# Taking the softmax remainder two pairs at a time, with the weighing four pairs behind the scores

## The chip, the cores and the metric

One core of one Trainium2 chip runs the whole program. The metric is device microseconds (us) of one execution. TensorE is called PE here, VectorE DVE, ScalarE ACT, GpSimd POOL, and SyncE, which issues most of the DMAs, SP.

## The reference

Two graph layers over 4096 rows of 128 features, each with a residual and a layernorm:

```
norm2 = ||x|| by row                              # (4096, 1)
cos   = beta * (x @ x.T) / (norm2 @ norm2.T + 1e-7)
P     = softmax(cos + (1 - adj) * -1e9, axis=1)   # adj: 4096 x 4096 of 0 and 1, with its diagonal
x     = layernorm(x + P @ x)
x     = layernorm(x + adj @ (x @ weight))
```

## The kernel before

The first layer works in 8 blocks of 512 output rows (`b`), and in each block over the 4096 columns of the graph in 16 **pairs** of 128-column tiles (`m`); `n = 16 b + m` counts the 128 pairs. Everything is held transposed: one pair is a tile of 128 partitions by 2 x 512 columns. Sums run in float16 with a high part and a remainder ("lo"), so that they keep the precision of float32. For one pair:

1. `scores(b, m)` on PE: six matmuls of 512 columns (L854 to L856) into one of two PSUM buffers `S`. It waits until the exponential of pair n-2 has been taken.
2. `exp_pair` on ACT (L424): `E[slot] = exp(scale * S)`, float32, 1024 columns. `E`, `eh` and `el` are rings of RING = 4 slots, one for each pair. It waits for the remainder of pair n-4 (`lo_done`), which still reads the slot of `E`.
3. `mask_pair` on DVE (L639): E times a power of two, minimum with the bytes of the transposed adjacency (`adjT`), in place.
4. `split_hi` on ACT (L433): `eh[slot]` = E in float16. It waits for the weighing of pair n-4 (`pv_done`).
5. `split_lo` on DVE (L647): `el[slot]` = E minus `eh`, in float16: the **remainder**.
6. `weigh` on PE (L877, L881): sixteen matmuls, eight of 257 columns with `eh` and eight of 129 with `el`, add the pair into the four PSUM banks `O`. It waits for `lo_done` of the pair.

Each engine runs its own program in the order in which it is written, and waits on semaphores between. In one step `m` PE does `scores(b, m)` and then `weigh` of the pair LAG = 3 behind; ACT does `exp_pair(b, m)` and then `split_hi(b, m-1)`; DVE does `mask_pair(b, m)` and then `split_lo(b, m-1)`.

The end of block b-1 is worked in among the steps of block b. At step LAG, ACT copies a part of `O` out (`read_out`, L449) and DVE adds the rest (L685, `o_read`); PE weighs nothing at that step's turn and, one step later, weighs pair 0 (which waits for `o_read`) and pair 1. DVE then spreads small instructions over the steps: `scale_den` at step 3, `residual` (L698) at 4 and 5, `row_moments` (L652) at 6 and 7, `norm_stats` (L659 to L677) at 8. POOL takes a power (`power`, L376) of what `norm_stats` leaves, and DVE's `row_shift` (L709) at step 10 waits for it. ACT's `normalise` (L460), one tile at each of the steps 11 to 14, waits for `row_shift` before its first tile, and `split_x1_hi` (L469) at step 15 lets POOL subtract the high part of the result (`x1p`, L388).

POOL also starts the DMAs that turn the float32 adjacency into bytes in DRAM (`cast`, L353), and its queue is served in order, so a `power` stands behind the casts in front of it. SP transposes the bytes into `adjT` (L258, L264). Each of the two waits for the other's last pieces.

The second layer starts when the last pair is weighed: `aggregate` (L935) on PE, 64 fp8/float16 matmuls of 512 columns for each block, and `weights` (L945). At the end of the first layer PE weighs the last LAG pairs one after the other and goes straight to `aggregate`.

Of the kernel before, what the change touches and what calls it, by code (L numbers as in the profile page):

```python
# [11 lines left out]
ALU = mybir.AluOpType  # L12
# [9 lines left out]
def resnorm_graph_kernel(nc, x, adj, beta, weight, x1_dram, x1p_dram, q_dram, adj8_dram, out):  # L22
# [10 lines left out]
    NT = N // P  # L33
    NP = NT // 2
    NPAIR = NB * NP
    LAG = 3
    RING = 4
    XC = 2 * D + 1
    HB = BI // 2
# [11 lines left out]
    with ExitStack() as ctx:  # L51
# [3 lines left out]
        def sem(name):  # L55
            return ctx.enter_context(nc.semaphore(name))
# [101 lines left out]
        lo_done = sem("lo_done")  # L158
# [238 lines left out]
        def _(act):  # L397
# [43 lines left out]
            def read_out(b):  # L441
                if later(b):
                    act.wait_ge(o_read, 2 * b)
                for half in range(2):
                    if half == 0:
                        act.wait_ge(half_weighed, b + 1)
                    else:
                        act.wait_ge(pv_done, (b + 1) * NP)
                    nc.scalar.activation(o_lo[:, half * HT:(half + 1) * HT, :],  # L449
                                         psum[:, 4 + half * HT:4 + (half + 1) * HT, D:XC],  # L450
                                         ACT.Copy).then_inc(o_lo_read, 1)
# [28 lines left out]
            for b in range(1, NB):  # L480
                for m in range(NP):
                    if m == LAG:
                        read_out(b - 1)
# [25 lines left out]
        def _(dve):  # L509
# [24 lines left out]
            def uT_lo_part(g):  # L534
                dve.wait_ge(uT_hi, g + 1)
                nc.vector.tensor_tensor(uT_out(1, g), uT_in(g), uT_out(0, g), ALU.subtract).then_inc(uT_lo, 1)
# [61 lines left out]
            def add_small_term(b, m):  # L598

                n = b * NP + m  # L600
                dve.wait_ge(s_filled, n + 1)
                dve.wait_ge(q_row_in, 16 * (b + 1))
                if later(b) or m >= RING:
                    dve.wait_ge(lo_done, n - RING + 1)
                for a in range(2):
                    num, den = E[:, m % RING, a, 0:HB], E[:, m % RING, a, HB:BI]
                    for half in range(2):
                        base = 16 * n + 8 * a + 4 * half
                        part = slice(half * HB, (half + 1) * HB)
                        rows = q_row[:, part].rearrange("q (r p) -> q p r", r=2)  # L610
                        nc.vector.tensor_scalar_mul(num.rearrange("q (p r) -> q p r", r=2), rows,
                                                    q[:, 2 * m + a:2 * m + a + 1]).then_inc(fix, 1)
                        dve.wait_ge(fix, base + 1)
                        nc.vector.tensor_scalar_add(den, num, EPS_COS).then_inc(fix, 1)
                        dve.wait_ge(fix, base + 2)
                        nc.vector.reciprocal(den, den).then_inc(fix, 1)
                        dve.wait_ge(fix, base + 3)
                        nc.vector.tensor_tensor(num, num, den, ALU.mult).then_inc(fix, 1)
                        dve.wait_ge(fix, base + 4)
                        s = S[m % 2][:, a, part]  # L620
                        done = nc.vector.tensor_tensor(s, s, num, ALU.mult)
                        if half == 0:
                            done.then_inc(half_scaled, 1)
                            dve.wait_ge(half_scaled, 2 * n + a + 1)
                        elif a == 1:
                            done.then_inc(scaled, 1)

            def mask_pair(b, m):

                n = b * NP + m  # L630
                dve.wait_ge(e_done, n + 1)
                if not later(b) and m < 3:
                    dve.wait_ge(first_in[m], 16)
                elif m == 0:
                    dve.wait_ge(piece_in[0], 16 * b)
                elif m % (NP // MP) == 0:
                    dve.wait_ge(piece_in[m // (NP // MP)], 16 * (b + 1))
                e = E[:, m % RING, :, :]
                nc.vector.scalar_tensor_tensor(out=e, in0=e, scalar=EPRE, in1=mask_bytes(b, m), op0=ALU.mult,  # L639
                                               op1=ALU.min).then_inc(masked, 1)  # L640

            def split_lo(b, m):

                n = b * NP + m
                dve.wait_ge(hi_done, n + 1)
                s = m % RING
                nc.vector.scalar_tensor_tensor(out=el[:, s, :, :], in0=E[:, s, :, :], scalar=ECAST, in1=eh[:, s, :, :],  # L647
                                               op0=ALU.mult, op1=ALU.subtract).then_inc(lo_done, 1)

            def moments(src, o, ts, base):  # L650
                for t in ts:
                    last = nc.vector.bn_stats(stats[:, o + t, :], src(t))  # L652
                if IT - 1 in ts:
                    last.then_inc(chain, 1)
# [38 lines left out]
            def residual(b, ts):  # L693
                dve.wait_ge(o_read, 2 * (b + 1))
                dve.wait_ge(chain, 6 * b + 2)
                dve.wait_ge(xres_in, 16 * (b + 1))
                for t in ts:
                    last = nc.vector.scalar_tensor_tensor(out=h[:, t, :], in0=h[:, t, :], scalar=rden[:, t:t + 1],  # L698
                                                          in1=xres[:, t, :], op0=ALU.mult, op1=ALU.add)
                if IT - 1 in ts:  # L700
                    last.then_inc(chain, 1)

            def row_moments(b, ts):
                dve.wait_ge(chain, 6 * b + 3)
                moments(lambda t: h[:, t, :], 0, ts, 6 * b + 3)
# [11 lines left out]
            def xaug_lo(c):  # L717
                dve.wait_ge(x_hi, c + 1)
                nc.vector.scalar_tensor_tensor(out=xaug[:, chunk(c), D + 1:XC], in0=xfull[:, chunk(c), :],
                                               scalar=col(C_XS), in1=xaug[:, chunk(c), 0:D], op0=ALU.mult,  # L720
                                               op1=ALU.subtract).then_inc(x_lo, 1)

            def layer(tiny):
                for m in range(NP):
                    if tiny:
                        add_small_term(0, m)
                    mask_pair(0, m)
                    if m % 2 == 0 and m < 2 * NC:
                        xaug_lo(m // 2)
                    if m in (1, 2):  # L730
                        uT_lo_part(UG // 2 + 2 * m - 2)
                        uT_lo_part(UG // 2 + 2 * m - 1)
                    if m > 0:
                        split_lo(0, m - 1)
                def block_of_rows(b):
                    for m in range(NP):
                        if m == LAG:
                            read_out(b - 1)
                        if tiny:
                            add_small_term(b, m)  # L740
                        mask_pair(b, m)
                        split_lo(b, m - 1)
                        if m == 3:
                            scale_den(b - 1)
                        if m in (4, 5):
                            residual(b - 1, range(2 * m - 8, 2 * m - 6))
                        if m in (6, 7):
                            row_moments(b - 1, range(2 * m - 12, 2 * m - 10))
                        if m == 8:
                            norm_stats(b - 1)  # L750
                        if m == 10:
                            row_shift(b - 1)

                if tiny:
                    with dve.Fori(1, NB) as b:
                        block_of_rows(b)
                else:
                    for b in range(1, NB):
                        block_of_rows(b)
                split_lo(NB, -1)  # L760

            with dve.If(small < 1):
                layer(False)
# [3 lines left out]
            b = NB - 1  # L767
# [56 lines left out]
        def _(pe):  # L824
# [69 lines left out]
            def weigh_lagged(b, m):  # L894
                weigh(b * NP + m - LAG, (m - LAG) % NP)

            for m in range(NP):
# [11 lines left out]
                if m == 0:  # L909
                    pe.wait_ge(norms, 1)  # L910
                    pe.wait_ge(uT_lo, 4)
                    nc.tensor.transpose(q_turned, q[:, :], ident[:, :]).then_inc(q_filled, 1)
                if m == LAG:

                    pe.wait_ge(uT_lo, UG)
                if m >= LAG:
                    if (m - LAG) % (CT // 2) == 0:
                        pe.wait_ge(x_lo, (m - LAG) // (CT // 2) + 1)
# [74 lines left out]
```

## Time and profile before

| | |
|---|---|
| time, median of 3 runs | 515.58 us (515.1 to 516.22) |
| the profiled execution's own time | 515.68 us |
| its span in the profile | 513.8 us |
| busy: PE, DVE, ACT, POOL | 469.7, 380.6, 314.2, 64.8 us |
| first layer's pairs | to about 389 us |
| second layer | from about 389 us |

The profiled execution lies 0.1 us from the median, so its trace can stand for the runs. Busy times are over the whole span; DVE and ACT have little to do in the second layer, where PE works alone. In the rows further down a start is in us from the span's start, and the idle time in brackets is that of the row's own engine before the instruction, with what ended it.

### The profile page before, as it was taken

The numbers are of one execution on the slowest core, as the hardware profiler recorded it, in microseconds if no ns is written. First come the engines' busy times: TensorE is split into PE (matmuls) and PEld (weight loads), VectorE is DVE, ScalarE is ACT, GpSimd is POOL, SyncE is SP. The second block draws the span as 40 slices with busy tenths as digits, with TensorE's granted clock in tenths as the row PEclk, the third lists the DMA queues.
The fourth block names the chain that finished last, engine by engine and source line by source line (L and its number), as shares of the span: only waits on it lengthen the run. The fifth ranks groups of instructions, "written<-read, shape, count | busy, mean of one in ns | idle before, by whom it ended". The sixth has DMA issues, their size and how long they took to land.

```text
span 513.8 us, 8872 instructions
## 1 busy us (share of the span) xinstructions
PE 469.7 (91%) x3491; PEld 305.1 (59%) x3491; DVE 380.6 (74%) x630; ACT 314.2 (61%) x358; POOL 64.8 (13%) x71
## 2 busy tenths in 40 slices
PE   0866999957999999999999999999999999999995
PEld 0533676635676666766666767666665455544584
DVE  4976989928999999999999999999994022212253
ACT  3665888828879978988988997898891000000000
POOL 3500000010101201201120210110101000000011
PEclk9988999997999999999999999999999999999998
DMA  5899899999999999999989979520024101111111
GB/s 189 62 101 127 86 122 115 137 127 115 172 127 135 131 136 118 131 169 115 112 171 114 105 152 104 93 74 7 1 51 156 63 5 37 41 43 41 42 37 46
DMA packets 101690, 50.20 MB, mean 98 GB/s; under 512 B 69376, under 2 KB 98208, under 8 KB 101664
## 3 DMA queue, kind: packets, MB, share of 16 engines
q0 software_dynamic: 17952, 16.78, 39.5%
q1 hardware_dynamic: 83424, 33.05, 30.2%
q8 instruction: 11, 0.18, 0.1%
q14 instruction: 15, 0.12, 0.1%
q10 hardware_dynamic: 288, 0.07, 0.1%
HBM read 77.40 MB, written 22.82 MB: 195 GB/s over the span
## 4 chain that ended last, share of the span: by engine, by line
PE 66%; DMA 20%; DVE 4%; issue 4%; ACT 3%; POOL 1%; POOLq 0%; ACTq 0%; DVEq 0%
PE psum L935 21%; PE psum L877 16%; DMA adj_bytes<-in_adj 12%; PE psum L881 8%; DMA adjT<-adj_bytes 7%; PE psum L854 7%; PE psum L856 7%; PE psum L855 7%; DVE E L639 2%; ACT E L424 1%; PE psum L945 1%; DMA adjT<-in_x 1%; ACT eh L433 1%; DVE el L647 1%; POOL rn L360 1%
## 5 line engine op out<-in xcount | busy, mean ns | idle before, releaser
L877 PE MATMUL psum<-xaug,eh 128*128 128x257 f16 x1024 | 187.9, 277 | 22.5 <-DVE el L647 15.4
L424 ACT ACTIVATE E<-psum,sc 128x1024 f32<-128x1024 f32 x128 | 154.1, 1204 | 54.8 <-PE psum L856 50.6
L881 PE MATMUL psum<-xaug,el 128*128 128x129 f16 x1024 | 178.7, 223 | 0.0
L639 DVE SCALAR_TENSOR_TENSOR E<-E,adjT 128x1024 f32<-128x1024 f32 x128 | 160.0, 1250 | 21.1 <-ACT E L424 13.0
L647 DVE SCALAR_TENSOR_TENSOR el<-E,eh 128x1024 f16<-128x1024 f32 x128 | 156.5, 1223 | 0.1
L433 ACT ACTIVATE eh<-E 128x1024 f16<-128x1024 f32 x128 | 134.0, 1047 | 3.8 <-DVE E L639 3.8
L877 PEld LDWEIGHTS psum<-xaug,eh 128*128 128x128 f16 x1024 | 100.3, 99 | 52.3 <-DVE el L647 16.9
L935 PE MATMUL psum<-adjT,uT 128*128 128x512 fp8e4 (+1 forms) x576 | 112.1, 355 | 0.0
L881 PEld LDWEIGHTS psum<-xaug,el 128*128 128x128 f16 x1024 | 101.4, 99 | 13.4
L854 PE MATMUL psum<-uT 128*128 (+1 forms) x256 | 98.4, 384 | 0.0
L855 PE MATMUL psum<-uT 128*128 (+1 forms) x256 | 97.8, 382 | 0.0
L856 PE MATMUL psum<-uT 128*128 (+1 forms) x256 | 97.5, 381 | 0.0
L935 PEld LDWEIGHTS psum<-adjT,uT 128*128 128x128 f16 x576 | 56.4, 98 | 53.0
L501 ACT ACTIVATE E<-psum 128x512 f32<-128x512 f32 x7 | 4.2, 597 | 88.0 <-PE psum L935 88.0
L792 DVE TENSOR_TENSOR E<-psum,E 128x512 f32<-128x512 f32 x7 | 4.8, 690 | 68.1 <-PE psum L945 68.1
L376 POOL TENSOR_TENSOR rstd<-rstd,half_pow 128x4 f32<-128x4 f32 (+1 forms) x17 | 22.2, 1304 | 186.1 <-DVE rstd L677 186.1
L353 POOL DMA_DIRECT2D adj_bytes<-in_adj x31 | 19.6, 631 | 192.1 <-DMA adjT<-adj_bytes 192.1
L856 PEld LDWEIGHTS psum<-uT 128*128 128x128 f16 x256 | 25.3, 99 | 31.0 <-issue 1.4
L854 PEld LDWEIGHTS psum<-uT 128*128 128x128 f16 x256 | 25.4, 99 | 17.9 <-issue 0.7
L855 PEld LDWEIGHTS psum<-uT 128*128 128x128 f16 x256 | 25.3, 99 | 16.4 <-issue 0.5
L460 ACT ACTIVATE x<-h,shift,rstd 128x128 f32<-128x128 f32 x32 | 15.2, 482 | 16.6 <-DVE shift L709 16.6
L388 POOL TENSOR_TENSOR x1p<-x,x1p 128x512 f16<-128x512 f32 x7 | 12.4, 1764 | 58.6 <-ACT x1p L469 58.6
(71 smaller groups left out, 159.9 us busy)
## 6 DMA issues: line engine op xcount, KB each, us to landing
adj_bytes<-in_adj POOLq DMA_DIRECT2D x31, 512.0 KB, 11.1
adjT<-in_x SPq DMA_DIRECT2D x4, 512.0 KB, 8.6
xres<-in_x SPq DMA_DIRECT2D x8, 256.0 KB, 5.3
q_row<-norms SPq DMA_DIRECT2D x8, 256.0 KB, 4.9
x_rows<-x SPq DMA_DIRECT2D x8, 256.0 KB, 3.6
E<-x_rows SPq DMA_DIRECT2D x8, 256.0 KB, 3.0
out<-E SPq DMA_DIRECT2D x16, 128.0 KB, 2.2
x_parts<-x1p SPq DMA_DIRECT2D x7, 256.0 KB, 5.5
```

The lines of the kernel that those rows point to most:

```text
L353: pool.dma_start(piece(adj8_v, b, c), piece(adj_v, b, c)).then_inc(piece_cast[c], 16)
L376: nc.gpsimd.tensor_tensor(rstd[:, o:o + n], rstd[:, o:o + n], half_pow[:, 0:n], ALU.pow).then_inc(rstd_done, 1)
L424: nc.scalar.activation(E[:, m % RING, :, :], S[m % 2], ACT.Exp, bias=col(C_BB), scale=col(C_BS)).then_inc(e_done, 1)
L433: nc.scalar.activation(eh[:, m % RING, :, :], E[:, m % RING, :, :], ACT.Copy, scale=ECAST).then_inc(hi_done, 1)
L639: nc.vector.scalar_tensor_tensor(out=e, in0=e, scalar=EPRE, in1=mask_bytes(b, m), op0=ALU.mult, op1=ALU.min).then_inc(masked, 1)
L647: nc.vector.scalar_tensor_tensor(out=el[:, s, :, :], in0=E[:, s, :, :], scalar=ECAST, in1=eh[:, s, :, :], op0=ALU.mult, op1=ALU.subtract). ...
L854: nc.tensor.matmul(o, hj, hi, start=True, stop=False)
L855: nc.tensor.matmul(o, hj, li, start=False, stop=False)
L856: last = nc.tensor.matmul(o, lj, hi, start=False, stop=True)
L877: return nc.tensor.matmul(O[t][:, 0:XC], eh[:, s, a, cols], xaug[:, j, :], start=start, stop=stop)
L881: return nc.tensor.matmul(O[t][:, 0:D + 1], el[:, s, a, cols], xaug[:, j, 0:D + 1], start=False, stop=False)
L935: last = nc.tensor.matmul(out, x1p_all[:, j, part * D:(part + 1) * D], adj_cols(r, j, cols), start=j == 0 and part == 0, stop=j == NT - 1 ...
```

## The change

`LAG` goes from 3 to 4, while the rings keep 4 slots. `split_lo` now takes the remainder of two pairs in one instruction of 2048 columns, at even steps only: at step m (even) it covers pairs m-2 and m-1, and raises `lo_done` by 2. The small instructions of the row end are set to other steps: `scale_den` 4, `residual` 5 and 7, `row_moments` 8 and 9, `norm_stats` 9, `row_shift` 11. `read_out` moves with LAG, from step 3 to 4, on ACT and on DVE, and so do PE's empty turn (4) and double turn (5). ACT's `normalise` stays at steps 11 to 14.

```
-    LAG = 3
+    LAG = 4
     RING = 4
...
                 dve.wait_ge(hi_done, n + 1)
-                s = m % RING
+                s = slice((m - 1) % RING, (m - 1) % RING + 2)
                 nc.vector.scalar_tensor_tensor(out=el[:, s, :, :], in0=E[:, s, :, :], scalar=ECAST, in1=eh[:, s, :, :],
-                                               op0=ALU.mult, op1=ALU.subtract).then_inc(lo_done, 1)
+                                               op0=ALU.mult, op1=ALU.subtract).then_inc(lo_done, 2)
...
-                    if m > 0:
+                    if m > 0 and m % 2 == 0:
                         split_lo(0, m - 1)
...
                         mask_pair(b, m)
-                        split_lo(b, m - 1)
-                        if m == 3:
+                        if m % 2 == 0:
+                            split_lo(b, m - 1)
+                        if m == 4:
                             scale_den(b - 1)
-                        if m in (4, 5):
-                            residual(b - 1, range(2 * m - 8, 2 * m - 6))
-                        if m in (6, 7):
-                            row_moments(b - 1, range(2 * m - 12, 2 * m - 10))
-                        if m == 8:
+                        if m in (5, 7):
+                            residual(b - 1, range(m - 5, m - 3))
+                        if m in (8, 9):
+                            row_moments(b - 1, range(2 * m - 16, 2 * m - 14))
+                        if m == 9:
                             norm_stats(b - 1)
-                        if m == 10:
+                        if m == 11:
                             row_shift(b - 1)
```

## Rows read from the trace of the kernel before

**Rows 1.** The page's groups: busy us, mean ns, then idle before and its releaser.

```profile
L639 DVE SCALAR_TENSOR_TENSOR E<-E,adjT 128x1024 f32<-128x1024 f32 x128 | 160.0, 1250 | 21.1 <-ACT E L424 13.0
L647 DVE SCALAR_TENSOR_TENSOR el<-E,eh 128x1024 f16<-128x1024 f32 x128 | 156.5, 1223 | 0.1
...
L698 DVE SCALAR_TENSOR_TENSOR h<-h,rden,xres 128x128 f32<-128x128 f32 x32 | 9.6, 345 | 0.1
...
L685 DVE TENSOR_TENSOR h<-psum,o_lo 128x256 f32<-128x256 f32 x16 | 6.0, 416 | 3.6 <-issue 3.6
```

**Rows 2.** Who waited for whom: us in total, times, longest us.

```profile
PE psum L877 <- DVE el L647: 15.4, 4, 8.9
...
PE psum L877 <- DVE h L685: 2.3, 7, 0.9
```

**Rows 3.** The chain that ended last, in pieces: start us, us, what.

```profile
118.44 0.40 PE psum L877
...
304.03 0.23 PE psum L856
...
346.60 0.23 PE psum L856
...
385.30 2.06 DVE el L647
...
388.92 27.69 PE psum L935 x128
```

**Rows 4.** Timeline of PE: a weighing after a wait, and one followed by scores.

```profile
46.92 0.39 PE L877 MATMUL psum<-xaug,eh 128*128 128x257 f16 x1 [4.86 <-DVE el L647]
...
290.90 0.27 PE L877 MATMUL psum<-xaug,eh 128*128 128x257 f16 x1
...
292.24 0.38 PE L854 MATMUL psum<-uT 128*128 x1
```

**Rows 5.** Timeline of ACT: the exponential and the first normalised tile.

```profile
116.14 0.49 ACT L460 ACTIVATE x<-h,shift,rstd 128x128 f32<-128x128 f32 x1 [9.51 <-DVE shift L709]
116.54 1.19 ACT L424 ACTIVATE E<-psum,sc 128x1024 f32<-128x1024 f32 x1
...
291.24 1.20 ACT L424 ACTIVATE E<-psum,sc 128x1024 f32<-128x1024 f32 x1
...
299.15 1.21 ACT L424 ACTIVATE E<-psum,sc 128x1024 f32<-128x1024 f32 x1
...
381.65 1.21 ACT L424 ACTIVATE E<-psum,sc 128x1024 f32<-128x1024 f32 x1
```

**Rows 6.** Timeline of DVE: masks, remainders and the row end.

```profile
43.31 1.23 DVE L639 SCALAR_TENSOR_TENSOR E<-E,adjT 128x1024 f32<-128x1024 f32 x1 [7.67 <-DMA adjT<-adj_bytes]
...
115.95 0.16 DVE L709 SCALAR_TENSOR_TENSOR shift<-mean,rstd 128x4 f32<-128x4 f32 x1 [10.27 <-POOL rstd L376]
...
117.16 1.22 DVE L647 SCALAR_TENSOR_TENSOR el<-E,eh 128x1024 f16<-128x1024 f32 x1
118.30 1.22 DVE L639 SCALAR_TENSOR_TENSOR E<-E,adjT 128x1024 f32<-128x1024 f32 x1
...
279.13 0.48 DVE L652 BATCH_NORM_STATS2 stats<-h 128x6 f32<-128x128 f32 x2
...
281.79 0.15 DVE L659 TENSOR_TENSOR tmp<-stats 128x4 f32<-128x4 f32 x1
...
282.56 1.22 DVE L639 SCALAR_TENSOR_TENSOR E<-E,adjT 128x1024 f32<-128x1024 f32 x1
...
300.38 1.83 DVE L639 SCALAR_TENSOR_TENSOR E<-E,adjT 128x1024 f32<-128x1024 f32 x1 [0.27 <-ACT E L424]
```

**Rows 7.** Timeline of POOL: a power, and the remainder of the result.

```profile
114.87 1.04 POOL L376 TENSOR_TENSOR rstd<-rstd,half_pow 128x4 f32<-128x4 f32 x1
...
299.27 1.86 POOL L388 TENSOR_TENSOR x1p<-x,x1p 128x512 f16<-128x512 f32 x1 [12.16 <-ACT x1p L469]
```

**Rows 8.** Windows of 1 us, one of them: busy by engine, granted clock (PEclk), DMA.

```profile
47.00:48.00 1.00, 1.00 (x7) 0.81 (x8) 1.00 (x2) 0.76 (x1) 0.00 (x0) 0.50 1.06 93
```

## The prediction, on record before the changed kernel ran

> **What bounds the kernel now.** I read the page first, then the waits, the chain, the windows, and last the timelines of each engine around a block's end. The page shows DVE busy at every pair, yet with idle time in front of the masks that ACT's exponential ended 13.0 us of [rows 1]: DVE is not the bound of the steady part. The pace is PE's. Exponentials run three pairs apart at 291.24 and 299.15, 2.637 us a pair [rows 5]; a weighing takes 292.24 - 290.90 = 1.34 [rows 4], which leaves 1.30 for the scores, and PE is at work all that time. From block to block the chain repeats every 346.60 - 304.03 = 42.57 us [rows 3], that is 16 x 2.637 = 42.19 and 0.38 in which PE waits for DVE's read-out (seven such waits, 2.3 us, the longest 0.9 [rows 2]). Time not spent at this pace lies at the start, where casts and transposes come late: a mask waits 7.67 us for its DMA at 43.31, and at 115.95 `row_shift` has waited 10.27 us for POOL's power [rows 6], which started at 114.87 [rows 7], right behind a cast that a DMA held. PE starts again at 118.44 [rows 3]. So three things can matter: what DVE's new order makes PE wait for, the read-out, and the end of the layer.
>
> **The merged instruction, by itself.** Two remainders that follow without a wait start 1.14 apart (117.16 to 118.30 is one remainder and the next mask) [rows 6]. From 128 to 1024 columns such an instruction grows by 1223 - 345 = 878 ns over 896 columns [rows 1], or 1.00 us for 1024 more: 2.14 us from start to next start. With no saving at all it would be 2.28. I take 2.20, the middle. At best this frees 64 x 0.14 = 9 us of DVE, at worst none, and none of it lies on the path: while PE sets the pace it is worth 0. If DVE were the bound, that would be the gain. Here a rule speaks against the change: the Trainium skill, "Perfetto Trace Analysis", section "Optimizing Scalar/DVE Operations", says that grouping helps a saturated engine, with about 60 ns of access overhead for each DVE operation, and that breaking instructions up may finish work sooner where the engine isn't saturated but holds another up. By its 60 ns the merge would give 64 x 0.06 = 3.8 us if DVE were saturated and nothing as it is; the trace agrees that DVE is not.
>
> **The steady pace.** Call X(n) the start of exp n. The mask follows after 1.23 (299.15 to 300.38), the double remainder 1.14 later, and PE can weigh 1.28 + 1.06 = 2.34 after its start (117.16 to 118.44 was 1.28 [rows 3, 6]). The first of the two pairs is ready at X(n) + 4.71. PE wants it at X(n+2) less 0.34 (290.90 against 291.24 [rows 4, 5]) = 4.93. It holds, by 0.22 us. That is all the slack there is: DVE late by more than this at an even step stalls PE.
>
> **Blocks 2 to 7, steps 8 to 14: the loss.** The row end now falls so that a chain passes through DVE, ACT and DVE again. From X(8): mask 8 at 1.23, remainder (6, 7) at 2.37, over at 4.57; `row_moments` 0.48 [rows 6], 5.05; mask 9, 6.19; `row_moments` 0.48 and `norm_stats` 0.77 (281.79 to 282.56), 7.44; this is 0.94 late for mask 10, whose exp is ready at 5.27 + 1.23 = 6.50. Mask 10, 8.58; remainder (8, 9), 10.78; mask 11, 11.92; only now `row_shift`. ACT has exp 12 behind `normalise`, which waits for that: 0.19 to the tile, 0.40 to exp 12 (115.95, 116.14, 116.54 [rows 5, 6]), 12.51. DVE has nothing between, since step 11 is odd. Mask 12 at 13.74, remainder (10, 11) at 14.88, PE can weigh pair 10 at 17.22. PE wants it at 6 x 2.637 - 0.34 = 15.48. The stall is 1.74 us (0.6 of it already before pair 8). With 2.14 and 2.28 for the three double remainders it is 1.56 and 1.98. After it there is slack again: exp 14 to 16 and normalise fit in PE's pace. Before the change `row_shift` stood one step earlier, with a remainder behind it, and cost nothing. Six blocks: **+10.4** (9.4 to 11.9). POOL's power starts one step later, still some 3 us ahead of `row_shift`; the casts behind it move by as much, and after block 2 no mask waits for them. SP's queue waits for masks and for x1, not for remainders.
>
> **Block ends.** While POOL subtracts x1p (299.27, 1.86 us [rows 7]) the mask at 300.38 takes 1.83 instead of 1.22 [rows 6]. That was hidden. Now it is mask 16, an even one, so pairs 14 and 15 are ready at 1.23 + 1.75 + 2.34 = 5.32, against 4.93: 0.39 us, in five blocks **+2.0**. Bounds: 0, if POOL's instruction falls elsewhere, and 3, if it lies over more.
>
> **The read-out** moves a step later, and PE gets the scores of one more pair in front of the weighing that waits. From X(2): remainder (0, 1) over at 4.57, mask 3 at 5.71, read-out 0.42 [rows 1], 6.13; PE wants it at 5.27 - 0.34 + 1.30 = 6.23. No wait: five blocks give back 0.38, block 2 its 0.9: **-2.8** (at least -2.3).
>
> **The start.** In block 0 the mask at 43.31 now has two remainders behind it, one of which (pair 2) had been taken earlier. PE resumes 1.06 later and with a weighing of 1.34 undone: 2.4 us late. But block 1 ends at POOL's power, at 115.95, which hangs on DMAs, and PE was idle for 8.9 us there [rows 2]. The delay goes into that idle time. From there: exp 12 at 116.54 as before, scores 14 at once at half clock (as behind the idle time at 46.92: clock 0.50 [rows 4, 8]), mask 12, the remainder of 10 and 11, PE's weighing of 10 at about 121.3, done 122.6. Before, both were done at 122.6 too. **0** (to +1, if the clock comes back later).
>
> **The end of the layer.** Before, from the last exp at 381.65 to the first `aggregate` at 388.92 it took 7.27 [rows 3, 5]. Now, from X(127): the remainder (124, 125) is over at 4.57 - 2.64 = 1.93, the mask runs from there, and the last remainder starts 2.41 after the mask's start (before: 382.88 to 385.30) or when POOL's x1p is over: the row at 385.30 took 2.06, 0.84 too long, which puts that at 4.49. PE weighs pair 126 at 6.83, then 1.34 and 1.51 for the last: 9.68, less 1.34 because one weighing more lies behind the last scores. **+1.1** (0.8 to 1.4). PE idles about 3.1 us there; 4.9 us idle brought half the clock [rows 4, 8]. If 3.1 do so too, 1.5 more.
>
> **Sum:** 10.4 + 2.0 - 2.8 + 0 + 1.1 = +10.7 on the profiled execution's 515.68: **526.4 us**. Median and profiled execution differ by 0.1.
>
> **Rivals.** (a) *Faster.* PE feels nothing of the chain through `row_shift`, and what shows is the read-out: 515.7 - 2.8 + 1.1 = 514.0. It decides if the 17.22 fall below 15.48. Every link has a duration in the trace and the order of both engines forbids going round it. 4 in 100. (b) *A smaller loss.* Mask 10 isn't late, since DVE's small instructions close up, and x1p misses mask 16: the stall is 1.74 - 0.94 = 0.80, six times 4.8, in all 515.7 + 4.8 - 2.8 + 1.1 = 518.8. Against it stands that `row_moments` and `norm_stats` have those times in the rows. 11 in 100, of which 3 for no measurable change. (c) *A larger loss.* The sync at 115.95 does not absorb the 2.4 us of the start, because DMAs wait for compute after all, and the clock falls at the layer's end: 526.4 + 2.4 + 1.5 = 530.3, more if x1p takes 3. For it: nothing in SP's or POOL's queue before 115 that I find. 10 in 100. (d) *The merge doesn't shorten DVE's work*: in the range (1.98 a block). The forecast itself has 75.
>
> **Range.** The bounds of the terms give 9.4 + 0 - 2.8 + 0 + 0.8 = +7.4 and 11.9 + 3 - 2.3 + 1 + 1.4 = +15.0. I widen the low end toward (b): 520.5 to 531. A measurement can tell about 0.2%, 1 us. Slower 93 in 100, same 3, faster 4.
>
> **What would show it.** Block period in the chain about 44.3 us instead of 42.57. PE waits for L647 rise by six stalls of 0.6 and of 1.1 us and five of 0.4. Exp 12 waits for `shift` L709 in blocks 2 to 7, and mask 12 for exp 12, about 1.8 us each. PE's waits for L685 go to about nothing after block 1. The power at about 115 keeps its time. L647: 64 instructions of about 2.3 us. Wrong would be: no wait at exp 12, a steady part that is no longer at 2.637 a pair, or a first resumption of PE after 119.

## The result, and the profile after

The changed kernel takes 524.38 us (median of 4 runs, 523.47 to 526.12) against 515.34 us for the kernel before: ratio 1.0183, 95% interval 1.0146 to 1.022. It is slower by 9.0 us, where 10.7 was forecast. The profiled execution took 523.47, with a span of 521.7.

The page's groups for the changed kernel. PE's lines have moved by one (L877 is L878 now):

```profile
L878 PE MATMUL psum<-xaug,eh 128*128 128x257 f16 x1024 | 187.0, 276 | 23.2 <-DVE el L647 21.9
L639 DVE SCALAR_TENSOR_TENSOR E<-E,adjT 128x1024 f32<-128x1024 f32 x128 | 157.7, 1232 | 39.3 <-ACT E L424 31.8
...
L647 DVE SCALAR_TENSOR_TENSOR el<-E,eh 128x2048 f16<-128x2048 f32 x64 | 146.2, 2285 | 1.2 <-ACT eh L433 1.2
```

The 64 double remainders save 10.3 us of DVE's busy time against [rows 1], and DVE waits 18.8 us longer for exponentials. Who waited for whom (us, times, longest):

```profile
DVE E L639 <- ACT E L424: 31.8, 43, 1.7
ACT x L460 <- DVE shift L709: 26.2, 8, 8.4
...
PE psum L878 <- DVE el L647: 21.9, 18, 5.7
```

PE waited for remainders 4 times before [rows 2], 18 times now. The chain, in pieces (start us, us, what), gives the block's period and the start of `aggregate`:

```profile
279.24 0.23 PE psum L857
...
323.10 0.23 PE psum L857
...
396.85 27.63 PE psum L936 x128
```

A block takes 43.86 us, 1.67 over PE's 42.19, against 42.57 before [rows 3]; `aggregate` starts 7.93 later. Timeline of DVE at steps 8 to 12 of one block, and around mask 16:

```profile
284.21 0.48 DVE L652 BATCH_NORM_STATS2 stats<-h 128x6 f32<-128x128 f32 x2
284.61 1.21 DVE L639 SCALAR_TENSOR_TENSOR E<-E,adjT 128x1024 f32<-128x1024 f32 x1
285.73 0.48 DVE L652 BATCH_NORM_STATS2 stats<-h 128x6 f32<-128x128 f32 x2
...
287.02 1.22 DVE L639 SCALAR_TENSOR_TENSOR E<-E,adjT 128x1024 f32<-128x1024 f32 x1
288.16 2.29 DVE L647 SCALAR_TENSOR_TENSOR el<-E,eh 128x2048 f16<-128x2048 f32 x1
290.36 1.22 DVE L639 SCALAR_TENSOR_TENSOR E<-E,adjT 128x1024 f32<-128x1024 f32 x1
291.50 0.15 DVE L709 SCALAR_TENSOR_TENSOR shift<-mean,rstd 128x4 f32<-128x4 f32 x1
293.31 1.23 DVE L639 SCALAR_TENSOR_TENSOR E<-E,adjT 128x1024 f32<-128x1024 f32 x1 [1.66 <-ACT E L424]
294.45 2.29 DVE L647 SCALAR_TENSOR_TENSOR el<-E,eh 128x2048 f16<-128x2048 f32 x1
...
301.50 1.22 DVE L639 SCALAR_TENSOR_TENSOR E<-E,adjT 128x1024 f32<-128x1024 f32 x1
303.65 1.23 DVE L639 SCALAR_TENSOR_TENSOR E<-E,adjT 128x1024 f32<-128x1024 f32 x1 [0.93 <-ACT E L424]
```

ACT in the same block, and the last exponential of the layer:

```profile
291.69 0.49 ACT L460 ACTIVATE x<-h,shift,rstd 128x128 f32<-128x128 f32 x1 [2.00 <-DVE shift L709]
292.09 1.19 ACT L424 ACTIVATE E<-psum,sc 128x1024 f32<-128x1024 f32 x1
...
387.51 1.21 ACT L424 ACTIVATE E<-psum,sc 128x1024 f32<-128x1024 f32 x1 [0.32 <-PE psum L857]
```

And PE: the two restarts that belong to those steps (pairs 8 and 10), with the read-out wait of block 2 in front.

```profile
138.45 0.28 PE L878 MATMUL psum<-xaug,eh 128*128 128x257 f16 x1 [1.24 <-DVE h L685]
...
290.50 0.29 PE L878 MATMUL psum<-xaug,eh 128*128 128x257 f16 x1 [0.51 <-DVE el L647]
...
296.79 0.29 PE L878 MATMUL psum<-xaug,eh 128*128 128x257 f16 x1 [0.85 <-DVE el L647]
```

In the kernel before, the same links stood like this (DVE, then ACT): the mask follows `row_shift` at once, and the tile at 288.02 comes 0.9 us after it and has not waited.

```profile
287.10 0.15 DVE L709 SCALAR_TENSOR_TENSOR shift<-mean,rstd 128x4 f32<-128x4 f32 x1
287.21 1.23 DVE L639 SCALAR_TENSOR_TENSOR E<-E,adjT 128x1024 f32<-128x1024 f32 x1
...
288.02 0.48 ACT L460 ACTIVATE x<-h,shift,rstd 128x128 f32<-128x128 f32 x1
```

In the changed kernel this is the chain to read in order: mask 11 at 290.36, `row_shift` at 291.50, the normalised tile at 291.69, exp 12 at 292.09, mask 12 at 293.31, double remainder at 294.45, PE at 296.79. DVE stands idle for 1.66 us in the middle of it. The same two waits, 0.51 and 0.84 or 0.85 us, stand in each of blocks 2 to 7; each restart loses a little more than the idle time shown, 1.67 in all by the period.

### The profile page after: what moved, and what is told of

It is laid out like the page before. It is cut to its first block, busy times and chain, and to the rows that moved or that the text cites. A ratio compares the mean times of both kernels' runs of the same rounds, so it can differ in the third digit from the quotient of the medians.

```text
span 521.7 us, 8878 instructions
## 1 busy us (share of the span) xinstructions
PE 474.0 (91%) x3491; PEld 304.8 (58%) x3491; DVE 373.2 (72%) x566; ACT 313.3 (60%) x358; POOL 60.9 (12%) x71
## 4 chain that ended last, share of the span: by engine, by line
PE 54%; DMA 20%; DVE 16%; ACT 4%; issue 4%; POOL 1%; POOLq 0%; ACTq 0%; DVEq 0%
PE psum L936 21%; PE psum L878 12%; DMA adj_bytes<-in_adj 11%; DVE el L647 9%; DMA adjT<-adj_bytes 8%; PE psum L882 6%; PE psum L857 5%; PE psum L855 5%; PE psum L856 5%; DVE E L639 4%; ACT E L424 4%; PE psum L946 1%; DMA adjT<-in_x 1%; DVE stats L652 1%; POOL rn L360 1%
## 5 line engine op out<-in xcount | busy, mean ns | idle before, releaser
L878 PE MATMUL psum<-xaug,eh 128*128 128x257 f16 x1024 | 187.0, 276 | 23.2 <-DVE el L647 21.9
L639 DVE SCALAR_TENSOR_TENSOR E<-E,adjT 128x1024 f32<-128x1024 f32 x128 | 157.7, 1232 | 39.3 <-ACT E L424 31.8
L647 DVE SCALAR_TENSOR_TENSOR el<-E,eh 128x2048 f16<-128x2048 f32 x64 | 146.2, 2285 | 1.2 <-ACT eh L433 1.2
L878 PEld LDWEIGHTS psum<-xaug,eh 128*128 128x128 f16 x1024 | 100.0, 99 | 56.6 <-DVE el L647 25.7
L855 PE MATMUL psum<-uT 128*128 (+1 forms) x256 | 99.4, 388 | 5.1 <-ACT E L424 5.1
L856 PE MATMUL psum<-uT 128*128 (+1 forms) x256 | 99.2, 388 | 0.0
L857 PE MATMUL psum<-uT 128*128 (+1 forms) x256 | 99.0, 387 | 0.0
L833 PE MATMUL psum<-ident,adjT 128*128 128x128 f32 x32 | 6.6, 367 | 12.1 <-DVE adjT L530 12.1
```

The source lines that it names most:

```text
L855: nc.tensor.matmul(o, hj, hi, start=True, stop=False)
L856: nc.tensor.matmul(o, hj, li, start=False, stop=False)
L857: last = nc.tensor.matmul(o, lj, hi, start=False, stop=True)
L878: return nc.tensor.matmul(O[t][:, 0:XC], eh[:, s, a, cols], xaug[:, j, :], start=start, stop=stop)
```

## The experiments

Each was run beside the kernel before; ratios are to its runs on the same chip: 515.81 us in the median for the first four experiments, 514.65 for the last four. So times of the two groups are compared by their ratios. "A block" is one of blocks 2 to 7, by its period less 42.19 (the kernel before: 0.38).

**`row_shift` back at step 10.** One step of the changed kernel is edited.

```
-                        if m == 11:
+                        if m == 10:
                             row_shift(b - 1)
```

> The changed kernel with row_shift back at step 10, behind the double remainder (8, 9); nothing else moves. Theory A (the chain that holds exp 12 behind row_shift behind mask 11 makes most of the loss, on top of mask 10 being late): exp 12 starts about 0.9 us late instead of 1.8, the stall in front of pair 10 goes, that in front of pair 8 (0.5 to 0.7) stays; each of blocks 2 to 7 loses 0.7 instead of 1.67, so 524.4 - 5.8 = about 518.6 us. Rival B (the double remainder by itself makes PE wait, wherever the row end stands): 524, as the changed kernel. Rival C (only the late mask 10 costs, exp 12 is hidden): 524, as the changed kernel.

518.82 us, ratio 1.0052 (1.0021 to 1.0084). PE's timeline, two blocks in a row:

```profile
288.34 0.28 PE L878 MATMUL psum<-xaug,eh 128*128 128x257 f16 x1 [0.51 <-DVE el L647]
...
331.18 0.28 PE L878 MATMUL psum<-xaug,eh 128*128 128x257 f16 x1 [0.50 <-DVE el L647]
```

Only the wait before pair 8 is left, at a period of 42.84: 0.65 a block, 1.02 less than in the changed kernel. B and C fall for the wait before pair 10; whether the double remainder by itself causes the wait before pair 8 is left to the fourth experiment. More than half of the loss was `row_shift` standing one step too late.

**`normalise` one step later.** The same link, cut on ACT; DVE's order is the changed kernel's.

```
-                    if m in (11, 12, 13, 14):
-                        normalise(b - 1, [m - 11])
+                    if m in (12, 13, 14, 15):
+                        normalise(b - 1, [m - 12])
```

> The changed kernel with ACT's normalise at steps 12 to 15 instead of 11 to 14; DVE's order stays. Theory A: exp 12 no longer stands behind row_shift, so the stall in front of pair 10 goes, that in front of pair 8 stays (0.5 to 0.7), and ACT is up to 0.4 late at exp 16 (0.15 us of PE): about 0.85 a block instead of 1.67, so 519.5 us. The same link as in the run with row_shift at step 10, cut on the other engine. Rivals B and C: 524.

518.63 us, ratio 1.0058 (1.0034 to 1.0083). DVE's timeline shows the gap behind `row_shift` closed:

```profile
288.64 0.15 DVE L709 SCALAR_TENSOR_TENSOR shift<-mean,rstd 128x4 f32<-128x4 f32 x1
288.91 1.23 DVE L639 SCALAR_TENSOR_TENSOR E<-E,adjT 128x1024 f32<-128x1024 f32 x1
```

and PE's the wait before pair 8, 43.10 apart, 0.91 a block where 0.85 was expected:

```profile
287.64 0.28 PE L878 MATMUL psum<-xaug,eh 128*128 128x257 f16 x1 [0.51 <-DVE el L647]
...
330.74 0.28 PE L878 MATMUL psum<-xaug,eh 128*128 128x257 f16 x1 [0.51 <-DVE el L647]
```

What exceeds the 0.65 of the run above comes before pair 14: exp 16 starts 3.11 after exp 15 (295.89 to 299.00), and the double remainder behind it is late.

**The merge alone undone.** LAG 4 and the new steps stay.

```
-                s = slice((m - 1) % RING, (m - 1) % RING + 2)
+                s = m % RING
...
-                                               op0=ALU.mult, op1=ALU.subtract).then_inc(lo_done, 2)
+                                               op0=ALU.mult, op1=ALU.subtract).then_inc(lo_done, 1)
...
-                    if m > 0 and m % 2 == 0:
+                    if m > 0:
...
-                        if m % 2 == 0:
-                            split_lo(b, m - 1)
+                        split_lo(b, m - 1)
```

> The changed kernel with the merge alone undone: one remainder of 1024 columns at each step, LAG 4 and every small instruction where the changed kernel has it. Theory A: a single remainder is ready 3.9 us before PE wants it, so a late exp 12 and a late mask 10 cost nothing, and the read-out's wait stays away; against the kernel before: -1.9 (blocks 3 to 7), -0.9 (block 2), -1.3 (a weighing more lies behind the last scores), -0.6 (scores 14 start on exp 12 at the sync): about 511 us. Rival D (the new places of the row end cost by themselves, on ACT, merged or not): 520 or more.

521.44 us, ratio 1.0115 (1.0089 to 1.0142): a miss by 10 us, and rival D holds. PE waits for no remainder in blocks 2 to 7, as theory A had it, but its wait for the read-out has grown from 0.24 to 1.32. DVE's timeline:

```profile
249.55 0.15 DVE L709 SCALAR_TENSOR_TENSOR shift<-mean,rstd 128x4 f32<-128x4 f32 x1
251.35 1.23 DVE L639 SCALAR_TENSOR_TENSOR E<-E,adjT 128x1024 f32<-128x1024 f32 x1 [1.65 <-ACT E L424]
...
261.19 1.91 DVE L639 SCALAR_TENSOR_TENSOR E<-E,adjT 128x1024 f32<-128x1024 f32 x1 [0.20 <-ACT E L424]
263.02 1.21 DVE L647 SCALAR_TENSOR_TENSOR el<-E,eh 128x1024 f16<-128x1024 f32 x1
...
270.97 0.74 DVE L685 TENSOR_TENSOR h<-psum,o_lo 128x256 f32<-128x256 f32 x2
```

and PE's: the weighing that waits for it:

```profile
271.44 0.28 PE L877 MATMUL psum<-xaug,eh 128*128 128x257 f16 x1 [1.32 <-DVE h L685]
```

The 1.65 us behind `row_shift` are the same. The remainders then have slack, but the read-out of the next block, eight instructions of DVE after mask 16, has none. ACT's steps with a tile to normalise are 2.43 us long when they run without a wait (tiles at 249.74, 252.17, 254.59 and 257.01), so only 0.2 of lateness is won back in each; mask 16 loses 0.7 to POOL's x1p; and from 261.19 to the read-out DVE works without a gap and is still late. What I had called slack held for the weighings alone. A block is 1.45 over PE's pace (271.44 to 315.08, less 42.19). With the row end one step earlier it is 0.38 (the run with LAG 4 alone, below), so the late row end costs 1.07 with single remainders; the late `row_shift` cost 1.02 with the merge. What changes is which of PE's waits shows it.

**The merge with the row end spread.**

```
                         mask_pair(b, m)
+                        if m == 12:
+                            row_shift(b - 1)
                         if m % 2 == 0:
                             split_lo(b, m - 1)
...
-                        if m == 9:
+                        if m == 10:
                             norm_stats(b - 1)
-                        if m == 11:
-                            row_shift(b - 1)
```

and `normalise` at 12 to 15, as above.

> The changed kernel, merge kept, with the row end spread so that nothing is late: norm_stats at step 10 behind the double remainder, row_shift at step 12 between mask 12 and the double remainder, normalise at steps 12 to 15. Theory A: no stall of over 0.2 us in a block, 524.4 - 6 x 1.5 = about 515.4 us, as the kernel before: the merge gives nothing and takes nothing once the row end is out of its way. Rival B: 522 to 524.

514.17 us, ratio 0.9963 (0.993 to 0.9996). PE's timeline has one wait of 0.79 between 137 and 379 us and no other over 0.12:

```profile
172.91 0.28 PE L878 MATMUL psum<-xaug,eh 128*128 128x257 f16 x1 [0.79 <-DVE el L647]
...
379.55 0.28 PE L878 MATMUL psum<-xaug,eh 128*128 128x257 f16 x1 [1.03 <-DVE el L647]
384.17 0.29 PE L878 MATMUL psum<-xaug,eh 128*128 128x257 f16 x1 [1.77 <-DVE el L647]
```

A block is 0.22 over PE's pace (42.41), less than the 0.38 of the kernel before: the loss in the blocks was the row end's steps, and the double remainder alone makes no wait before pair 8. What stays are the two waits at the layer's end, 1.03 and 1.77. The interval ends just below 1, and the ten runs lie between 508.81 and 516.14, so no gain is claimed from it.

**The merge with LAG 3.**

```
-    LAG = 4
+    LAG = 3
```

> The changed kernel with LAG 3 instead of 4: the merge without the longer lag. PE wants pair n-2 (even n) at step n+1, 2.3 us after exp n, and the double remainder is ready 4.71 after exp n: PE waits 2.4 us in every second step, two pairs take 7.7 us instead of 5.27, and some 100 pairs behind the DMA-bound start make 515.8 + 120 = 635 us or more (up to 665 if the first two blocks lengthen too). If the merge needs no longer lag (rival: ACT and DVE run far enough ahead), it stays near 524.

669.37 us in one run. PE waits at every second step, 7.71 us apart inside a block:

```profile
210.88 0.28 PE L878 MATMUL psum<-xaug,eh 128*128 128x257 f16 x1 [2.24 <-DVE el L647]
...
218.59 0.28 PE L878 MATMUL psum<-xaug,eh 128*128 128x257 f16 x1 [2.26 <-DVE el L647]
```

The period is the expected one. The total is 4 us over the range's end; PE's granted clock from 200 to 240 us was 0.91, which the sum had left out, but that it made the 4 us is not shown. The merge can't be had without the longer lag.

**LAG 4 alone, with `row_shift` at step 10.** The kernel with single remainders, and:

```
-                        if m in (5, 7):
-                            residual(b - 1, range(m - 5, m - 3))
-                        if m in (8, 9):
-                            row_moments(b - 1, range(2 * m - 16, 2 * m - 14))
-                        if m == 9:
+                        if m in (5, 6):
+                            residual(b - 1, range(2 * m - 10, 2 * m - 8))
+                        if m in (7, 8):
+                            row_moments(b - 1, range(2 * m - 14, 2 * m - 12))
+                        if m == 8:
                             norm_stats(b - 1)
-                        if m == 11:
+                        if m == 10:
                             row_shift(b - 1)
```

> LAG 4 alone: single remainders, and the row end at steps that bring row_shift back to 10 (scale_den 4, residual 5 and 6, row_moments 7 and 8, norm_stats 8, row_shift 10). Against the run with single remainders and row_shift at 11 only the places of the row end differ. If that run lost because the wait of exp 12 behind row_shift makes DVE late and single remainders win back only 0.2 us a pair until the read-out, which PE meets without slack: the read-out's wait falls from 1.32 to about 0.4 a block, and the time to 513.5. If a late read-out has another cause (LAG 4 with single remainders as such), it stays at 521.

511.44 us, ratio 0.9918 (0.9887 to 0.9948). The read-out's wait is back at 0.24 a block, and the period at 42.57. So what gave back the read-out's wait in the changed kernel was the merge's order (no remainder between mask 3 and the read-out), not the longer lag:

```profile
307.68 0.28 PE L877 MATMUL psum<-xaug,eh 128*128 128x257 f16 x1 [0.24 <-DVE h L685]
...
350.25 0.28 PE L877 MATMUL psum<-xaug,eh 128*128 128x257 f16 x1 [0.24 <-DVE h L685]
```

**Single remainders with the spread row end.** The kernel of the fourth experiment with the merge undone as in the third.

> The merged kernel with its row end spread (norm_stats 10, row_shift 12, normalise 12 to 15; 514.2 us), with single remainders instead of double ones and nothing else changed: what the merge itself is worth once the row end is out of its way. Read-out after mask 3 and remainder 2: ready 0.4 us too late in blocks 3 to 7, +2.0 against the merged one, and the end of the layer without waiting for a double remainder, -1.5: 514.5 us, the same within the measurement. If the merge's saved DVE time mattered, 517 or more.

514.33 us, ratio 0.9993 (0.997 to 1.0016). Beside 0.9963 for the merged one the intervals overlap: no gain of the merge can be told from these runs, though it leaves DVE 10 us less to do. The pair is not clean, however. With single remainders PE is done with the layer earlier, and `aggregate` then waits for a transfer of normalised rows, which SP starts only behind the last normalised tile of block 6, late in a spread row end. The critical chain and PE's timeline:

```profile
382.15 4.82 DMA uT<-x_parts
...
387.11 3.48 PE L935 MATMUL psum<-adjT,uT 128*128 128x512 fp8e4 x9 [2.39 <-DMA uT<-x_parts]
```

Behind the 2.39 us of idle time PE's granted clock was 0.50 from 388 to 391 us, and the first 128 matmuls of `aggregate` took 29.47 us, against 27.63 to 27.79 in the other kernels. The merged kernel starts `aggregate` at the same transfer, with only 0.34 of waiting: it had lost the time already.

**LAG 4 alone, with an earlier read-out.** The kernel of 511.44 us, with DVE's read-out between mask 3 and remainder 2.

```
-                        if m == LAG:
-                            read_out(b - 1)
...
                         mask_pair(b, m)
+                        if m == LAG - 1:
+                            read_out(b - 1)
                         split_lo(b, m - 1)
```

> LAG 4 alone (single remainders, row_shift 10) with DVE's read-out one instruction earlier, between mask 3 and remainder 2. o_lo is ready 2.6 us after exp 3, read-out done at 3.1, PE wants it at 3.58: no wait for it in any block, 0.4 x 5 less than with the read-out behind remainder 2: about 511.5 us, faster than both kernels by 0.8%.

509.64 us, ratio 0.9899 (0.9863 to 0.9935). PE's timeline has no wait at all between these two, from block 1 to the layer's end:

```profile
114.06 0.61 PE L854 MATMUL psum<-uT 128*128 x1 [8.28 <-ACT E L424]
...
378.73 0.28 PE L877 MATMUL psum<-xaug,eh 128*128 128x257 f16 x1 [0.57 <-DVE el L647]
```

This is the lowest median of the study, 1.0% under the kernel before by the ratio and 2.8% under the changed one (0.9899 / 1.0183). Its interval overlaps that of LAG 4 alone; that the read-out's wait is gone, and with it 0.38 a block, is shown by the trace.

**All of them without the start.** The profiled executions differ by up to 4.4 us in when `row_shift` of block 1 runs, in no order that follows the edits. From there to the first matmul of `aggregate`, in us:

| kernel | `row_shift` of block 1 | `aggregate` | between |
|---|---|---|---|
| before | 115.95 | 388.92 | 272.97 |
| changed | 114.64 | 396.85 | 282.21 |
| `row_shift` at 10 | 114.43 | 391.84 | 277.41 |
| `normalise` later | 114.43 | 391.66 | 277.23 |
| single remainders | 116.57 | 395.74 | 279.17 |
| merge, row end spread | 113.24 | 387.37 | 274.13 |
| LAG 4 alone | 114.32 | 385.73 | 271.41 |
| single, row end spread | 115.20 | 387.11 | 271.91 |
| earlier read-out | 112.22 | 380.24 | 268.02 |

The change loses 9.24 us here, and the spread row end takes back 8.08 of it. Beside its single twin the merge loses 2.22, of which the twin gives up 1.8 again in `aggregate` at half clock. LAG 4 alone gains 1.56 us, 0.3%; the rest of its 0.8% is not traced to a cause, and may be the start.

## Why the prediction was right, by its own steps

It forecast 526.4 and a loss of 10.7; the medians give 524.38 and 9.0. Of the two profiled executions, up to `aggregate`, the terms are:

| term | predicted | measured |
|---|---|---|
| steps 8 to 14, six blocks | +10.4 | 6 x 1.67 = +10.0 |
| x1p over mask 16 | +2.0 | 0 |
| read-out, blocks 3 to 7 | -1.9 | -1.9 |
| read-out, block 2 | -0.9 | 1.24 - 0.87 = +0.4 |
| start, absorbed at POOL's power | 0 | 0 |
| end of the layer | +1.1 | 9.34 - 7.27 - 1.34 = +0.7 |
| POOL's power, earlier, not by the change | not foreseen | -1.3 |
| sum | +10.7 | +7.9 (396.85 - 388.92 = 7.93) |

Part of the closeness is luck: x1p missing (2.0 too much) and block 2's read-out (1.3 too little) go opposite ways, and the -1.3 of the power is chance between two executions. Without it the terms give 9.2, near the 9.0 of the medians.

**The loss** came out link by link. From exp 8 to the weighing of pair 10 the sum was 17.22 us; the trace has exp 8 at 279.63 and PE at 296.79, 17.16. The double remainder starts the next instruction after 2.20 (288.16 to 290.36), the value taken. Undoing one link removed 1.02 us a block on DVE and 0.76 on ACT, and spreading the row end left 0.22 of 1.67, so here the cause is shown, not only argued. Mask 10 was late by 0.89 (287.02, with exp 10 at 284.90), where the sum had 0.94.

**The mis-sized term is x1p.** The step said that POOL's subtraction would lengthen mask 16, now even, and stall PE by 0.39 in five blocks. But step 15 has no remainder, so DVE waits for exp 16 behind mask 15 instead of working up to it. POOL's timeline:

```profile
302.53 1.21 POOL L388 TENSOR_TENSOR x1p<-x,x1p 128x512 f16<-128x512 f32 x1 [12.12 <-ACT x1p L469]
```

It took 1.21 us and not 1.86 [rows 7], and was nearly over when mask 16 started at 303.65, behind 0.93 of idle time; the mask took 1.23. So the stall of 0.39 a block measured 0. In block 2 it went the other way: a mask at 132.06 took 2.66, and the read-out behind it, for which a gain of 0.9 was forecast, lost 0.4. DVE's timeline, with `row_shift` of block 1 in front, then two rows of POOL's:

```profile
114.64 0.16 DVE L709 SCALAR_TENSOR_TENSOR shift<-mean,rstd 128x4 f32<-128x4 f32 x1 [6.35 <-POOL rstd L376]
...
132.06 2.66 DVE L639 SCALAR_TENSOR_TENSOR E<-E,adjT 128x1024 f32<-128x1024 f32 x1 [0.70 <-ACT E L424]
...
131.83 0.61 POOL L353 DMA_DIRECT2D adj_bytes<-in_adj  x1 [1.32 <-DMA adjT<-adj_bytes]
132.46 1.17 POOL L388 TENSOR_TENSOR x1p<-x,x1p 128x512 f16<-128x512 f32 x1
```

The Trainium skill, "SBUF — State Buffer", section "SBUF: two separate sides", says that a POOL instruction which reads SBUF and a DVE instruction with two inputs in SBUF exclude each other for their whole length, and that the one that starts first goes first. The trace agrees in the steady blocks: before, x1p came 0.38 behind a remainder and took 1.86, and the mask behind x1p took 1.83 [rows 6, 7]; now x1p comes when mask 15 has 0.2 to go, and takes 1.21. I should have asked who comes first. The row of block 2 doesn't fit as it stands: the mask starts 0.40 before x1p by the profile, and yet it is the mask that is held. POOL was issuing a cast until x1p began, but such an issue by itself lengthened no mask of these two traces, so why the mask was held there stays open.

**The start** was absorbed, as forecast: PE took up its work of block 0 2.34 after the start of the double remainder behind the late mask (44.02 to 46.36), with one weighing more to do, and met `row_shift` at POOL's power all the same. From `row_shift` to the end of scores 14 and the weighing of pair 10 it took 6.67 before, 6.63 now (119.93 + 1.34 - 114.64). **The end of the layer** is 0.4 cheaper because x1p was over before the last remainder, and the 3.1 us of idle time fell apart into 0.70 and 1.76, behind which the granted clock stayed at 1.00.

**A statement that did not hold beyond its case** is that after step 14 the lateness is gone. With the merge it was, since PE's own stalls gave DVE the time; with single remainders it lived on to the read-out. **Rivals:** (a) and (c) did not come; (b) had the right sign for x1p only. That the merge by itself gains nothing while PE sets the pace is borne out as far as the runs go: ratio 0.9963 with it and 0.9993 without, the second with the transfer's wait in it.

## What to carry to other kernels

When a chain goes DVE, ACT, DVE in one step, look for what DVE has to do between: a small instruction moved from a step with a long one behind it to a step with none turned a free wait into 1 us in each block. Slack has to be counted for each instruction that another engine waits for, not for each engine: the single remainders had 3.9 us by the sum, the read-out in the same queue none. Grouping instructions on an engine that is not the bound bought nothing here; the longer lag that it needed was ahead of the kernel before by 0.8% without it (0.3% by the trace behind the start). And before two variants are called equal, look at what ended each: here both ended at the same transfer.

## What the runs showed of the hardware

The start of block 1's `row_shift`, which a chain of casts and transposes sets, lay between 112.2 and 116.6 us in the profiled executions of the nine kernels of the table, whose casts and transposes are the same (with LAG 3 nothing waited for it). What comes behind it moves by as much, so 1 us can't be told from two profiles alone. The same x1p subtraction of POOL took between 1.15 us (`normalise` later, with no mask or remainder of DVE beside its start) and 1.86 us (before, 0.38 behind the start of a remainder). And PE's granted clock stayed at 1.00 behind an idle time of 1.76 us (changed kernel, 393.99), but was 0.50 for three microseconds behind one of 2.39 us (single, row end spread, 387.11).
